# A graph-attention kernel on one core: VectorE's messages moved ahead of the addition of the bias

## What is computed

```python
scores = jnp.einsum('ehc,ehc->eh', q[dst], k[src]) / np.sqrt(C) + edge_bias
seg_max = jax.ops.segment_max(scores, dst, num_segments=N)
ex = jnp.exp(scores - seg_max[dst])
denom = jax.ops.segment_sum(ex, dst, num_segments=N)
alpha = ex / denom[dst]
msgs = v[src] * alpha[:, :, None]
out = jax.ops.segment_sum(msgs, dst, num_segments=N)
```

## Time and profile before

| | before |
|---|---|
| median of 3 runs | 6202.45 us (6200.96 to 6206.25) |
| the profiled execution, device time | 6205.67 us |
| its span in the profile | 6203.9 us |
| busy share of the span | PE 85%, DVE 73%, POOL 72%, PEld 57%, ACT 37% |
| gathers of the attention, first and last start | 219.0 us and 2748.1 us |
| between them (219 to 2750 us) | 1568 gathers at a mean of 983 ns, 1568 memsets at 461 ns |

### The profile page before, as it was taken

One profiled execution on the slowest core, in us unless ns is written; L12 is line 12 of the kernel. 1 busy time (PEld: TensorE's weight loads), 2 busy tenths in 40 slices (PEclk: granted clock), 3 DMA queues, 4 the chain that ended last, 5 costly groups with the idle time before them and its releaser, 6 DMA issues. The chain is left out here.

```text
span 6203.9 us, 165021 instructions
## 1 busy us (share of the span) xinstructions
PE 5259.4 (85%) x49582; PEld 3541.0 (57%) x49582; DVE 4526.3 (73%) x13500; ACT 2295.7 (37%) x5686; POOL 4496.4 (72%) x6062
## 2 busy tenths in 40 slices
PE   3688888888888888874799699998899997699995
PEld 2355555555555555553577467675476765467674
DVE  7566666666666666668899688886488887788886
ACT  3333333333333333333344244443644443444442
POOL 2588888888888888867000198886298886588883
PEclk9655565555555655555677699999999999899997
DMA  4433333333333333324333443333433334533335
GB/s 134 137 100 99 100 99 99 99 99 100 99 98 100 99 99 99 99 80 134 110 92 95 122 117 112 112 117 99 136 113 114 114 112 106 179 112 114 114 111 163
DMA packets 542000, 688.39 MB, mean 111 GB/s; under 512 B 217072, under 2 KB 427905, under 8 KB 541722
## 3 DMA queue, kind: packets, MB, share of 16 engines
q0 software_dynamic: 140208, 338.71, 19.8%
q1 hardware_dynamic: 401692, 348.45, 18.8%
HBM read 619.25 MB, written 67.52 MB: 111 GB/s over the span
## 5 line engine op out<-in xcount | busy, mean ns | idle before, releaser
L730 POOL DMA_INDIRECT at_kv<-kv_tab,at_idx x1568 | 1541.5, 983 | 276.6 <-POOL at_rest L734 139.6
L2247 ACT ACTIVATE ag_msg<-ag_pair 128x768 bf16<-128x768 f32 x1200 | 944.2, 809 | 1371.1 <-PE ag_pair L2177 1298.5
L2186 PE MATMUL ag_sum<-ag_hot,ag_msg 128*128 128x240 bf16 x10800 | 1267.4, 267 | 1.1 <-DVE ag_msg L2116 0.7
L2186 PEld LDWEIGHTS ag_sum<-ag_hot,ag_msg 128*128 128x128 bf16 x10800 | 982.9, 98 | 334.0 <-issue 287.6
L2058 POOL DMA_INDIRECT ag_spill<-g_tab,ag_idx x600 | 587.2, 979 | 687.0 <-DMA ag_idx<-spill_tab 578.5
L2099 DVE TENSOR_SCALAR ag_hot<-iota_win,ag_node 128x240 bf16<-128x240 bf16 x4350 | 994.4, 339 | 0.0
L2067 POOL DMA_INDIRECT ag_spill<-g_tab,ag_idx x750 | 731.1, 975 | 126.3 <-POOL ag_rest L2070 80.9
L2177 PE MATMUL ag_pair<-xs,ag_pick 128*32 128x384 bf16 x14400 | 758.9, 330 | 67.3 <-issue 62.9
L734 POOL MEMSET at_rest<- 8x448 f32 x1568 | 723.2, 461 | 0.1
L2116 DVE CAST ag_msg<-ag_pair 128x768 bf16<-128x768 f32 x600 | 570.2, 950 | 131.5 <-PE ag_pair L2177 104.8
L2177 PEld LDWEIGHTS ag_pair<-xs,ag_pick 128*32 128x32 bf16 x14400 | 301.0, 96 | 330.0 <-issue 214.7
(11 more groups left out here) (333 smaller groups left out, 9313.9 us busy)
## 6 DMA issues: line engine op xcount, KB each, us to landing
ag_pick<-slot_tab SPq DMA_DIRECT2D x150, 768.0 KB
rk_hi_bc<-hi_tab SPq DMA_DIRECT2D x50, 896.0 KB
at_attr<-attr SPq DMA_DIRECT2D x196, 128.0 KB
at_qd<-q_tab SPq DMA_DIRECT2D x1568, 12.0 KB
at_kv<-kv_tab,at_idx POOLq DMA_INDIRECT x1568
ag_spill<-g_tab,ag_idx POOLq DMA_INDIRECT x1350
tr_dv<-dinv_tab SPq DMA_DIRECT2D x72, 256.0 KB
g_tab<-xs SPq DMA_DIRECT2D x48, 384.0 KB
```

The source lines that it names most:

```text
L730: nc.gpsimd.indirect_dma_start(kv[:, s.slot, ch, :], None, env["kv_tab"], bass.IndirectOffsetOnAxis(ap=idx[:, s.slot, ch:ch + 1], axis=0)) ...
L2186: last = nc.tensor.matmul(sum_ps[k][:, 0:WIN], row[:, part * DIM:(part + 1) * DIM], hot[:, k, ch, :], start=first and part == 0, stop=end ...
L2247: nc.scalar.activation(msg[:, p % 4, :, :], pair_ps[p % 3][:, :, 0:3 * DIM], ACT.Copy).then_inc(copied[p], 1)
```

## The change

In DVE's list of stages `messages` moves from behind `hot_one` to between `raise_max` and `add_bias`. The lags, the instruction, its operands, its waits and all lists of the other engines stay.

```diff
@@ -874,8 +874,8 @@
                 steps(dve, sh.BLOCKS, SLOTS, [
                     (3, run_max(0)), (3, run_max(1)), (3, own_max), (2, products), (3, above_score),
                     (4, scale_nodes), (4, load_bases), (3, node_max), (2, add_up), (3, load_first), (4, shrink),
-                    (3, raise_max), (2, add_bias), (4, merge), (0, place_one), (0, hot_one),
-                    (3, messages), (3, fall_short)], w)
+                    (3, raise_max), (3, messages), (2, add_bias), (4, merge), (0, place_one), (0, hot_one),
+                    (3, fall_short)], w)
```

## The result

| | before | with the change |
|---|---|---|
| median | 6204.35 us (6200.96 to 6207.54, 4 runs) | 6247.94 us (6243.86 to 6251.78, 4 runs) |
| span of the profiled execution | 6203.9 us | 6250.0 us |
| first to last gather's start | 2529.1 us | 2572.3 us |
| POOL's gathers in the attention | 1541.5 us, mean 983 ns | 1583.5 us, mean 1010 ns |

The changed kernel takes 1.007 times as long, with a 95% interval of 1.0053 to 1.0088: slower, where 6253 us and 0.8% were forecast. Of the 46.1 us that the span grew by, 43.2 lie between the first and the last gather, and 42.0 of these are gathers that POOL took longer over.

The account below looks back on a forecast made before the run. POOL's gathers and memsets were taken to bound the attention. Held gathers of 98.2 us less 46.2 gave +52 us, less 1 or 2 for quicker landings: 6253 us on the median, 0.8% slower, range 6212 to 6288 (own range 6235 to 6280).

Parts of the forecast that it names:

- POOL sets the pace: In the attention POOL's gathers and memsets bound each block, 12.6 us busy of 12.9; POOL never waits for a buffer.
- 1.1 us a block to spare: DVE and PE's loop waits about 1.1 us a block for gathers, so DVE delays up to that cost nothing.
- A gather is held while an instruction with two SBUF inputs runs: On POOL, gathers starting less than 1.09 us into DVE's messages are held until these end; 46.2 us now.
- The new place costs nothing in itself: Behind line 839 DVE idles 1.42 us until PE's bias; messages of 1.22 us fit there without delaying the bias.
- the old one gives nothing: At the messages' old place `fall_short` may go earlier, but DVE then waits for the maxima's broadcast; gain nothing.
- 98.2 us held less 46.2: POOL's gathers in the attention: holds expected at the messages' new place less those at the old, +52 us.
- 1 or 2 for gathers that land a little quicker: Taken off the +52 us: 1 or 2 us because gathers may land a little quicker at the slower pace.
- the rule: For gathers starting during the messages on DVE: excess is 1.09 us less the gather's offset from the messages' start.
- the forecast's count: For each of 196 blocks: line 839's start plus 0.21 us, next gather looked up, excess computed; 98.2 us together.
- A rival that came true in part: Gathers stretched much more, by starting early in the messages or by line 839 adding 0.28 us: 6313 us, chance 0.04.
- What would show it: Profile signs in the attention: mean gather 1015 ns, median 952, last gather 50 us later, longer DVE wait for gathers.

Follow-up runs that it names:

- the pair of runs in the same gap: Kernel before plus one DVE instruction with unread result at the messages' new place: a one-input reduction (ratio 1.0012) or a two-input multiplication (1.0092).

## Why the prediction was right, point by point

- *POOL sets the pace*: shown. In all twelve kernels with a memset of 448, 416 or 352 columns the time from the first to the last gather is the busy time of POOL's gathers and memsets plus 262.9 to 266.4 us (before: 2529.1 - 2264.7 = 264.4; after: 2572.3 - 2308.1 = 264.2), while the busy time itself goes from 2189 to 2326 us; and a shorter memset alone made the kernel faster. That DVE and PE have 1.1 us a block to spare for a real delay of the scores was not tested: no run with the usual rhythm delayed them.
- *A gather is held while an instruction with two SBUF inputs runs*: shown by the pair of runs in the same gap, and by the products of line 767, which have the operation and the size of half the messages, but one input in PSUM, and hold nothing.
- *The new place costs nothing in itself, the old one gives nothing*: right. The bias is added 1.70 us behind line 839 as before, and what was freed turned into waits ahead of lines 844 and 786. The wait for the bias fell to 54.1 us, with 40 forecast.
- *The size*: within the range, but one term was mis-sized. The forecast had +52 us, 98.2 us held less 46.2, and took off 1 or 2 for gathers that land a little quicker. Measured were 43.6 us between the medians and 43.2 between the first and last gather. Term by term: 90.8 us over 952 ns against 48.8, so +42.0; 4.7 of these are the median gather's 3 ns, and +37.3 are holds; the memsets gave +1.4.
- *The mis-sized term*: the rule held, but for gathers that start within 0.02 us of the messages' start: two do in the kernel before and aren't held, and only without them does it give the 46.2 us of the prediction, with them 48.3. Applied to all messages of the kernel after it gives 81.4 us, 16.8 less than forecast. What was off is where the messages fall: the next gather starts 0.71 us behind their start in the mean, where the forecast's count had 0.59. The landings moved as well. A block's second product, which waits for them, starts 2.98 us after the start of the block's last gather in the mean, where it was 3.10 before, while line 839 follows this product after 4.08 us in the median of both kernels. So the term at fault is the 1 or 2 us taken off for quicker landings, where the count came out 16.8 lower. That the landings make up the whole of the shift isn't shown, and why they come sooner was not tried. That the time lies closer to the forecast than the holds do is luck: the holds came to 37.3 us of 52, and 6.1 of the 43.2 us are the 3 ns of the median gather and the memsets' 1.4 us, which the forecast didn't have.
- *A rival that came true in part*: line 839, with two SBUF inputs itself, now stands right before the messages. In 4 of 196 steps a gather starts before it has ended and is held through the messages as well, for 1.1 to 1.2 us each, 4.6 us in all. The timeline of the kernel after has such a step:

```profile
1628.45 0.28 DVE L839 TENSOR_TENSOR aux<-aux,at_mnew 8x128 f32 x1
1628.53 2.17 POOL L730 DMA_INDIRECT at_kv<-kv_tab,at_idx  x1 [0.16 <-POOL at_rest L734]
1628.66 1.20 DVE L808 TENSOR_TENSOR at_msg<-at_kv,at_msg 128x1024 f32<-128x1024 f32 x1
```

- *What would show it*: the mean gather was forecast at 1015 ns and came to 1010, its median at 952 and came to 955, the last gather at 2798 and came at 2791.1, the wait for the gathers grew by 0.18 us a step, with up to 0.27 forecast.

## What to carry to other kernels

Filling an idle gap of one engine can cost time when the instruction put there holds up the engine that sets the pace. Look at the slowest instances of the bounding engine's instruction, not at their mean, and ask what ran when they started: here 0.25 us a block of held gathers was to be read from median, mean and maximum before anything was changed. When such a collision can't be avoided, cut the offending instruction into pieces with other work between them, each at a place where few of the other engine's instructions start; pieces side by side held as long as the whole.

## What the runs showed of the hardware that was not expected

- A gather that waits on POOL for a two-input instruction of DVE isn't let in between two such instructions that follow each other directly (0.89 us held, two halves of 0.67).
- A gather that starts almost together with the messages isn't held; the messages are. In the kernel before, gathers that started 0.01 and 0.02 us after the messages' start took their usual 0.95 us, and the messages 1.27 and 1.28 us instead of 1.22; one that started 0.05 us after it was held for 1.04 us.
- An indirect DMA issued on POOL took 1.63 us instead of 0.95 when it met an instruction of DVE with two SBUF inputs, while a one-input reduction in the same place left it at 0.95. The Trainium skill ("SBUF — State Buffer", section "Who interferes with whom") infers that such an instruction leaves descriptor generation alone; the measurement says otherwise for this DMA. Which part of the gather is held, the reading of the indices or another, no run separates.
- With the memset halved in all layers, so that gathers start every 1.39 us in the median instead of 1.57, the attention took 3010.7 us instead of 2529.1, with DVE waiting on signals that the profile calls remote; with the attention's memset at 381 ns instead of 461 it did not. The cause is open.
